# A two-layer transformer kernel whose planned order is rearranged in five places

## What is computed

```python
xn = layernorm(x)
x = x + attention(xn) + feed_forward(xn)
```

## Time and profile before

| | us |
|---|---|
| median of three runs | 607.77 |
| the profiled execution, its own time | 603.88 |
| its span, first to last instruction | 602.2 |
| TensorE (PE) busy | 566.0 |
| VectorE (DVE) busy | 456.7 |
| ScalarE (ACT) busy | 348.2 |
| GpSimd (POOL) busy | 234.2 |

### The profile page before, as it was taken

One profiled execution on the slowest core, in us unless ns is written; L12 is line 12 of the kernel. 1 busy time (PEld: TensorE's weight loads), 2 busy tenths in 40 slices (PEclk: granted clock), 3 DMA queues, 4 the chain that ended last, 5 costly groups with the idle time before them and its releaser, 6 DMA issues.

```text
span 602.2 us, 10503 instructions
## 1 busy us (share of the span) xinstructions
PE 566.0 (94%) x3216; PEld 435.4 (72%) x3216; DVE 456.7 (76%) x1232; ACT 348.2 (58%) x598; POOL 234.2 (39%) x345
## 2 busy tenths in 40 slices
PE   4899899999999999999999998989989999998997
PEld 3797567877777878668777676867667778775764
DVE  6499876856466687476898687798989889789673
ACT  3666746673564673675674666447645664556451
POOL 6143414623203421213223114354745486455242
PEclk9989999999999999999999999999999999999999
DMA  6987442244223244315434314335443354444101
GB/s 199 128 247 226 119 116 81 80 140 109 89 67 107 82 129 124 89 41 170 124 123 123 89 47 130 89 90 129 136 108 87 99 161 130 106 124 113 29 3 70
DMA packets 30535, 67.02 MB, mean 111 GB/s; under 512 B 4880, under 2 KB 18192, under 8 KB 28560
## 3 DMA queue, kind: packets, MB, share of 16 engines
q1 hardware_dynamic: 21840, 38.04, 24.3%
q0 software_dynamic: 8640, 28.32, 15.7%
HBM read 50.87 MB, written 13.63 MB: 107 GB/s over the span
## 4 chain that ended last, share of the span: by engine, by line
PE 69%; DVE 12%; issue 6%; DMA 5%; ACT 5%; POOL 2%; SPq 0%; DVEq 0%; ACTq 0%; POOLq 0%
PE banks L763 47%; PE banks L823 7%; PE banks L849 6%; PE banks L871 6%; DMA q_sb<-max_t 3%; DVE banks L1153 2%; DMA q_sb<-stage 1%; DVE x_res L1197 1%; ACT L1004 1%; DVE hid L1218 1%; PE banks L783 1%; PE banks L852 1%; POOL probs L705 1%; DVE bn L1051 1%; ACT hid_f L1005 1%
## 5 line engine op out<-in xcount | busy, mean ns | idle before, releaser
L985 ACT ACTIVATE probs<-banks 128x512 f32<-128x512 f32 (+1 forms) x256 | 138.0, 545 | 184.9 <-PE banks L849 150.1
L763 PE MATMUL banks<-xnT,w_up 128*128 128x512 f32 x576 | 151.6, 397 | 0.1
L1158 DVE TENSOR_REDUCE neg_max<-banks 128x2 f32<-128x512 f32 x128 | 87.5, 688 | 78.0 <-PE banks L823 76.2
L763 PE MATMUL banks<-w_down,hid 128*128 128x512 f32 x480 | 127.9, 400 | 5.7 <-ACT hid_f L1005 2.0
L763 PEld LDWEIGHTS banks<-xnT,w_up 128*128 128x128 f32 x576 | 101.6, 189 | 27.5 <-issue 10.3
L763 PEld LDWEIGHTS banks<-w_down,hid 128*128 128x128 f32 x480 | 85.3, 189 | 33.4 <-DVE neg_max L1158 8.9
L1153 DVE CUSTOM_DVE_ANT_0 banks<-banks,mask_qk 128x128 f32<-128x128 f32 (+1 forms) x256 | 86.4, 375 | 29.9 <-PE banks L823 29.4
L823 PEld LDWEIGHTS banks<-k_sb,q_sb 96*128 96x128 f32 x512 | 93.1, 193 | 22.0 <-issue 3.4
L823 PE MATMUL banks<-k_sb,q_sb 96*128 96x256 f32 (+1 forms) x512 | 100.4, 278 | 4.2 <-DMA q_sb<-stage 2.0
L705 POOL TENSOR_SCALAR_AFFINE_SELECT probs<-probs 128x256 f32<-128x256 f32 x128 | 61.8, 483 | 78.2 <-ACT probs L985 71.7
L849 PE MATMUL banks<-q_sb,k_sb 97*128 97x512 f32 x192 | 79.2, 412 | 9.9 <-DMA q_sb<-max_t 6.4
(11 more groups left out here) (79 smaller groups left out, 657.1 us busy)
## 6 DMA issues: line engine op xcount, KB each, us to landing
q_sb<-q_parts SPq DMA_DIRECT2D x60, 256.0 KB, 4.4
raw<-in_up POOLq DMA_DIRECT2D x48, 256.0 KB, 3.1
raw<-in_down POOLq DMA_DIRECT2D x40, 256.0 KB, 3.0
q_parts<-stage SPq DMA_DIRECT2D x30, 256.0 KB, 2.5
raw<-in_attn POOLq DMA_DIRECT2D x20, 256.0 KB, 3.6
k_parts<-stage SPq DMA_DIRECT2D x14, 256.0 KB, 2.5
k_sb<-k_parts SPq DMA_DIRECT2D x14, 256.0 KB, 4.0
out<-x_res SPq DMA_DIRECT2D x8, 256.0 KB, 2.2
```

The lines of the kernel that those rows point to most:

```text
L763: mm = nc.tensor.matmul(out_ap, lhs(a), rhs(b_), start=first and j == 0, stop=stop and j == 2, **kw)
L985: nc.scalar.activation(probs[:, i, 0:w], banks[:, ST_BANKS[k % 2], 0:w], ACT.Exp, scale=SCALES[n // B]).then_inc(exp_done, 1)
L1158: nc.vector.tensor_reduce(neg_max[:, s, 2 * g:2 * g + 2, t], banks[:, bank_of[x], :].rearrange("p (r t) -> p r t", r=2)[:, :, 0:w], AX.X, ...
```

## The change

Five edits. (1) `mt` and `mrow` join the head of slot 5: they are put into it directly behind `m`, and `with_followers` counts them as head, so that what is due in slot 5 comes behind them on every engine. TensorE has no part in what is due, so its order there stays. (2) In units 5, 9 and 13 the two output projection tiles stand behind the eight parts of `up` in `fill` and no longer in front; the second layer's units keep their order. (3) In unit 15 the key projection of batch 5 stands behind the four parts of its `up` and ahead of the downs. (4) The splits of the four w_out pieces, all in slot 7 of unit 0, go one each to slot 7 of units 0 to 3. (5) The first layer's keys are laid out by halves of four key heads (`k0` in `_layouts`), each on 64 partitions of the stage. For batch 0 SyncE issues the four transfers of the first half, the four of the queries of unit 0, the four of the keys' second half, and the four of unit 1's queries; scores of units 0 and 1 wait for the first half only. `qkv 0,1` on ScalarE waits for both halves. For batches 1 to 3 the addresses in DRAM follow the new layout.

```diff
--- before.py
+++ after.py
@@ -35,6 +35,7 @@
 CHUNKS = (2048 // P, 512 // P)
 PIECE = 512
 RAW = 4
+MT_SLOT = 5
 RING = 3
 ST_BANKS = (0, 1)
 WORK_BANKS = (2, 3, 4, 5, 7)
@@ -113,7 +114,7 @@
     due = [[] for _ in range(len(slots) + 5)]
     o = []
     for g, slot in enumerate(slots):
-        head = [k for k, x in enumerate(slot) if x[0] in ("st", "m")]
+        head = [k for k, x in enumerate(slot) if x[0] in ("st", "m", "mt", "mrow")]
         cut = head[-1] + 1 if head else 0
         for x in slot[:cut] + due[g] + slot[cut:]:
             o.append(x)
@@ -162,6 +163,8 @@
             slots[i].append(("m", u + 1, i + 4))
         if i >= 4 and u + 2 < UNITS:
             slots[i].append(("m", u + 2, i - 4))
+        if i == MT_SLOT and u + 1 < UNITS:
+            slots[i] += [("mt", u + 1), ("mrow", u + 1)]
     if s == 2 and n + 1 < 2 * B:
         slots[0].append(("load_k", n + 1, 0))
     if s == 0 and n > 0:
@@ -174,8 +177,6 @@
         slots[3] += [("norm", u - 1, 1), ("norm", u - 1, 2)]
         slots[4].append(("norm", u - 1, 3))
         slots[5].append(("ctx", u - 1))
-    if u + 1 < UNITS:
-        slots[5] += [("mt", u + 1), ("mrow", u + 1)]
     slots[5].append(("pv", u, 0))
     if s == 0 and n > 0:
         slots[2].append(("v", n))
@@ -224,20 +225,22 @@
             for t, i in enumerate((2, 3, 5, 6)):
                 slots[i] += parts(("down", 1, q, t))
     if s == 3 and n + 2 < 2 * B:
-        fill += parts(("qkv", n + 2, 2))
+        k = 4 if u == LU - 1 else len(fill)
+        fill[k:k] = parts(("qkv", n + 2, 2))
     if s == 0 and 0 < n < 2 * B - 1:
         fill += parts(("qkv", n + 1, 0))
     if s == 2 and n + 1 < 2 * B:
         fill += parts(("qkv", n + 1, 1))
     if s == 1 and n > 0:
-        fill = parts(("wo", n - 1, 0)) + parts(("wo", n - 1, 1)) + fill
+        k = 8 if u < LU else 0
+        fill = fill[:k] + parts(("wo", n - 1, 0)) + parts(("wo", n - 1, 1)) + fill[k:]
 
     if u < LU - 2:
         slots[4] += split(0, "up", 2 * u + 4, 2 * u + 5)
     if 0 < u < LU:
         slots[1] += split(0, "down", 2 * u, 2 * u + 1)
-    if u == 0:
-        slots[7] += split(0, "attn", 6, 7, 8, 9)
+    if u < S:
+        slots[7] += split(0, "attn", 6 + u)
     if LU - 6 <= u < LU - 3:
         k = (2, 0, 1)[u - (LU - 6)]
         slots[7] += split(1, "attn", 2 * k, 2 * k + 1)
@@ -445,7 +448,7 @@
         q_loaded = [sem(f"q_loaded{k}") for k in range(RING)]
         k_loaded = [sem(f"k_loaded{k}") for k in range(2)]
         m_loaded = [sem(f"m_loaded{k}") for k in range(RING)]
-        first_k = sem("first_k")
+        first_k = [sem(f"first_k{f}") for f in range(2)]
         first_q = [sem(f"first_q{j}") for j in range(2)]
         st_filled = sem("st_filled")
         exp_done = sem("exp_done")
@@ -483,7 +486,8 @@
         def wait_stage_free(eng, k):
 
             if k == 2:
-                eng.wait_ge(first_k, 64)
+                for f in range(2):
+                    eng.wait_ge(first_k[f], 64)
             elif k == 3:
                 for j in range(2):
                     eng.wait_ge(first_q[j], 64)
@@ -563,6 +567,14 @@
             def load_x(b):
                 sp_.dma_start(x_res[:, TT * b:TT * b + TT, :],
                               x_in[b].rearrange("(t p) d -> p t d", p=P)).then_inc(x_loaded[b], 16)
+
+            def first_keys(f):
+                k = stg[("store", 0, 2)]
+                for h in range(2):
+                    for e in range(2):
+                        at = 32 * h + 16 * e
+                        sp_.dma_start(k_sb[at:at + HD, 4 * f:4 * f + 4, :].bitcast(F32),
+                                      stage[64 * f:64 * f + 64, k % 2, h, 0, :].bitcast(F32)).then_inc(first_k[f], 16)
 
             for t in range(TT):
                 sp_.dma_start(x_res[:, t, :], x_in[0][t * P:t * P + P, :]).then_inc(x_loaded[0] if t else x_first, 16)
@@ -582,11 +594,7 @@
                     else:
                         sp_.wait_ge(staged_lo, rounds[("qkv", n, pair)] + 1)
                     if x == ("store", 0, 2):
-                        for h in range(2):
-                            for e in range(2):
-                                at = 32 * h + 16 * e
-                                sp_.dma_start(k_sb[at:at + HD, :, :].bitcast(F32),
-                                              stage[:, k % 2, h, 0, :].bitcast(F32)).then_inc(first_k, 16)
+                        first_keys(0)
                     elif x == ("store", 0, 0):
                         for j in range(2):
                             for e in range(2):
@@ -594,13 +602,18 @@
                                     at = 32 * e + 16 * h
                                     sp_.dma_start(q_sb[at:at + HD, j, :, :].bitcast(F32),
                                                   stage[:, k % 2, h, j, :].bitcast(F32)).then_inc(first_q[j], 16)
+                            if j == 0:
+                                first_keys(1)
                     elif pair < 2:
                         for j in range(2):
                             dst = qscr[n, 2 * pair + j].rearrange("(h d) (g t) -> (d g) h t", h=2, g=UH)
                             sp_.dma_start(dst, stage[:, k % 2, :, j, :].bitcast(F32)).then_inc(staged[k % 2], 16)
                     else:
                         for j in range(2):
-                            dst = kscr[n].rearrange("(h e) d (g t) -> e (d g) h t", e=2, g=NKV)[j]
+                            if n < B:
+                                dst = kscr[n].rearrange("q d x -> q (d x)").rearrange("(h e) (p t) -> e p h t", e=2, t=T)[j]
+                            else:
+                                dst = kscr[n].rearrange("(h e) d (g t) -> e (d g) h t", e=2, g=NKV)[j]
                             sp_.dma_start(dst, stage[:, k % 2, :, 0, :].bitcast(F32)).then_inc(staged[k % 2], 16)
                 if x[0] == "load_q":
                     u = x[1]
@@ -619,8 +632,12 @@
                     if n:
                         sp_.wait_ge(st_filled, st_index(S * (n - 1) + 2 * f + 1, 7) + 1)
                     g = slice(4 * f * T, (4 * f + 4) * T)
+                    if n < B:
+                        src = kscr[n].rearrange("q d x -> q (d x)").rearrange("q (f d x) -> f q d x", f=2, d=HD)[f]
+                    else:
+                        src = kscr[n].rearrange("q d x -> (q d) x")[:, g]
                     sp_.dma_start(k_sb[0:4 * HD, 4 * f:4 * f + 4, :].rearrange("p g t -> p (g t)").bitcast(F32),
-                                  kscr[n].rearrange("q d x -> (q d) x")[:, g]).then_inc(k_loaded[f], 16)
+                                  src).then_inc(k_loaded[f], 16)
                 if x[0] == "mrow":
                     u = x[1]
                     sp_.wait_ge(wk_emptied, em[("mt", u)] + 1)
@@ -817,7 +834,7 @@
                         if n:
                             pe.wait_ge(k_loaded[f], 16 * n)
                         else:
-                            pe.wait_ge(first_k, 64)
+                            pe.wait_ge(first_k[f], 64)
                     w = T if n < B or t == 1 else P
                     for r in range(2):
                         mm = nc.tensor.matmul(banks[:, k, r * T:r * T + w],
@@ -1237,7 +1254,8 @@
         return w.T.reshape(KT, P, -1).transpose(1, 0, 2)
 
     block = (REP + 2) * HD
-    w0 = np.concatenate([i["L0_attn_Wq"][q_rows(lambda h: h * HD)], i["L0_attn_Wk"][kd(lambda g: g * HD)],
+    k0 = np.array([(4 * f + g) * HD + d for f in range(2) for d in range(HD) for g in range(4)])
+    w0 = np.concatenate([i["L0_attn_Wq"][q_rows(lambda h: h * HD)], i["L0_attn_Wk"][k0],
                          i["L0_attn_Wv"][gd(lambda g: g * HD)]])
     rows1 = np.concatenate([q_rows(lambda h: (h // REP) * block + (h % REP) * HD),
                             kd(lambda g: g * block + REP * HD), gd(lambda g: g * block + (REP + 1) * HD)])
```

## The result

The changed kernel takes 611.22 us (median of 20 runs, 609.22 to 616.70) against 607.89 for the kernel before (20 runs). The ratio is 1.0075, 95% interval 1.0051 to 1.0099: slower, and outside the range of 599.0 to 607.5. The profiled execution took 610.63 us, its span is 608.9 instead of 602.2.

A forecast was written before the change was run, and what follows sets the result against it. TensorE was taken to bound the kernel, busy 566.0 of 602.2 us, with short stalls to remove. Gains of 11.55 us, kept at 85% (9.8), less 4.5 for the start, gave a 602.5 us median, range 600 to 605.5 (outer 599.0 to 607.5).

The forecast's parts named there:

- The start by halves: First keys: second half lands near 29.8 us, ScalarE waits for it, first scores come late; loss 4.5 us (2.7 to 8.2).
- (a): Rival, start is cheap: keys' second half lands by 28 us, loss 2.7 or less, 599.5 us; chance 0.19.
- (c): Rival, ScalarE held by the stage slot: half keys share engines with GpSimd's loads, loss 8.2, 610.6 us; chance 0.06.
- The rule of the Trainium skill: First keys: a transfer's increment lands only after the same DMA engine's earlier writes, so the second half follows the queries ahead.
- Splits: One w_out split per unit: the 1.84 us stall at `st 1,2` goes, 0.8 of a later one; gain 2.6 us.
- row of maxima: VectorE's copy into max_t goes ahead of adds, low parts and drains, so rows go out earlier; gain 2.8 us.
- banks: `mt`'s bank is free earlier, which cuts waits on `xnT` and `x_res`; gain 2.0 us (0 to 2.3).
- ups: Units 5, 9 and 13: ups ahead of output projection remove three stalls on hid_f; gain 1.95 us.
- unit 15: Key projection ahead of downs removes the 1.56 us wait of `down 15` and helps a later row; gain 2.2 us.
- (b): Rival, small stalls don't add up: backlog holds rows and banks, only 5.35 us gained against 4.5; 606.9 us; chance 0.2.
- The sum: Gains of 11.55 us kept at 85%, 9.8, less 4.5 for the start: span falls by 5.3 us.
- The check on idle time: Sign: the sum would be wrong if TensorE's idle time after 45 us did not fall from 25.3 to about 16.

The follow-up runs named there:

- experiment 6: experiment 5's kernel with batch 0's third projection staged in `probs`, so ScalarE isn't held by the keys' transfers: 600.13 us, ratio 0.9895 to the kernel before.
- experiment 1: The kernel before with edits 1 to 4 only, without the first layer's keys by halves: 595.67 us, ratio 0.9829 to the kernel before.
- experiment 5: The changed kernel with batches 1 to 3's keys half by half in DRAM, loaded over 64 rows, stored in four transfers: 600.56 us, ratio 0.9905 to the kernel before.
- experiment 12: experiment 1's kernel with the first row of maxima ahead of unit 2's queries in SyncE's queue: 590.48 us, ratio 0.9749 to the kernel before.

## Why the prediction was wrong, step by step

- **The start by halves** (-4.5): right in mechanism, in its times (`m 0,0` 32.96 for 32.3, `m 0,3` 36.59 for 36.1) and in size (3.0 to 4.6 us measured). At `st 0,0` the changed kernel is 3.4 us late. That the landing time was hit to 0.3 us is luck: the half landed at 30.14 here and at 28.1 to 29.4 in the six other profiles that have it. Rivals (a) and (c), which moved this term, both fail, (a) by little: it wanted the half by 28, (c) after 34. The rule of the Trainium skill that the prediction cites against this part agrees with the traces: in all seven the half lands 1.1 to 2.8 us behind the last increment of the queries ahead of it (30.14 for 28.00 here). What the step did not say is that ScalarE's hold is only the first of two limits there (experiment 6).
- **Splits, row of maxima, banks, ups, unit 15** (9.8 after 85%): right together, 10.4 us measured. The named stalls went as told, but for that of `st 31,0`, which stays at 0.30 us. Rival (b), small stalls that don't add up, gave 5.35 us; experiment 1 refutes it (8.0 to 12.8 us by its interval, 17.4 us idle instead of 25.3).
- **The sum** is the step that failed. It lacked a term, the load of the later keys over few DMA engines. The part on the first keys priced the four transfers of batch 0 and stopped there; the second half of edit 5, the addresses of the keys of batches 1 to 3 in DRAM, stands in the diff and in no sentence of the working, not even at nothing. It costs 10.3 us (experiment 5 against the change), as much as the four good edits bring. Had it stood beside the others at its measured size, the sum would be 4.5 + 10.3 - 9.8, 5 us slower; 3.3 was measured between the medians, 4.6 by the ratio.
- **The check on idle time** did its work: 25.8 us instead of 16 says at once that a new wait must exist, and the list of waits names it in its first line.

No view of the trace of before could show a load over four engines: each of its DMAs has 16 increments. But the earlier trace rows showed that a landing depends on what is queued ahead, and the diff showed the outermost dimension going from 64 to 4; with the rule cited above these two would have given the wait a place, if not its size.

Left open: the half clock from 552.0 to 555.4 in the changed kernel's profile. Only short waits stand ahead of it (0.98, 0.64 and 0.41 us from 547 on); experiment 1 has a half clock from 534 to 541 behind waits of 0.98 and 0.63 us at about the same place of the program, experiment 12 none there. Open too is what spreads the times of the kernel before (602 to 615 us in the 20 runs beside the changed kernel). The first row of maxima behind unit 2's queries may have a part, but the six runs of experiment 1, which has that wait, lie within 2.4 us, and the six of experiment 12 within 1.9; the reordering wasn't tried on the kernel before alone.

## What to carry to other kernels

Price every line of the diff, address patterns above all: a rearranged source or destination keeps its bytes and can lose three quarters of its DMA engines. In a queue with a deadline behind it, look at which transfer is ahead of the needed one; a landing time grows with what is queued, so a small urgent transfer goes ahead of a large one that isn't. And when edits are bundled, forecast and measure the good ones apart from the doubtful one: four of these are worth 1.7%, and the fifth costs more than that.

## What the runs showed of the hardware that was not expected

- A 256 KB load over four engines lands after 7.7 to 10.3 us, over sixteen after 3.5 to 5.0. It slows others as well, of GpSimd's queue too: two 256 KB loads in the same stretch went from 2.9 to 9.5 us (issues of 123.4 to 138 before, 123.2 to 138 after). Of the 16 increments of the first, 12 have come by 5.57 us and 4 come at 8.23 to 9.44. Not all of the 9.5 is due to the four engines, for these loads also stand nearer to the queries now; in experiment 5, where they do too, they take 5.8 us.

```profile
q_sb<-q_parts SPq DMA_DIRECT2D x2, 256.0 KB, 4.9
raw<-in_down POOLq DMA_DIRECT2D x2, 256.0 KB, 2.9
```
```profile
q_sb<-q_parts SPq DMA_DIRECT2D x2, 256.0 KB, 8.6
raw<-in_down POOLq DMA_DIRECT2D x2, 256.0 KB, 9.5
```

- A wait costs more than its length. Unit 4's 5.75 us came with 6.8 us at a granted clock of 0.50, and the step times put the unit at +8.8; unit 8's 2.88 us came with 3.4 us at 0.50, and +4.7. Against experiment 1, which has the four good edits too, the units are 7.9 and 4.7 us longer.
